# Four-layer decoder on one core: 128-column and 96-column TensorE products cut into column tiles of 64

## The reference

```python
# layer 0 attention: gates of 8 heads, from one small product
log_g = logsigmoid(x @ Wg + 6.906768)            # Wg: 256 x 8

# cross-attention of layers 0, 2 and 3: 16 heads, K=128, D_C=64, D_CQ=192, R=64
q_big  = einsum('bshk,hkq->bshq', hidden_q @ Wq.T, w_kc_q)   # rope on q_big in layers 0 and 2, not in 3
scores = einsum(q_big @ W_qr, kv_r @ W_kr)       # so W_qr . W_kr (192 x 64 per head) can be made first
attn   = softmax(scores); ctx_c = attn @ kv_r; out = (ctx_c @ w_kc_kv) @ Wo.T

# feed-forward of layers 1, 2, 3: the router
logits = x @ router                              # 256 x 16, 256 x 9, 256 x 8
```

## Time and profile before

| | |
|---|---|
| median of 3 runs | 1659.71 us |
| the profiled execution's own time | 1663.67 us |
| its span, first to last instruction | 1661.9 us |
| PE busy | 1621.5 us, 98% of the span |
| PE weight loads busy | 1098.9 us, 66% |
| DVE / ACT / POOL busy | 1114.3 / 750.1 / 239.8 us |
| mean granted TensorE clock | 0.994 |

### The profile page before, as it was taken

The page is one execution under the profiler, slowest core; times in us unless marked ns, Lnnn a source line. Parts: engine busy times, 40 slices in busy tenths (PEclk is TensorE's granted clock), DMA queues, the critical chain, the costliest instruction groups (busy, mean ns, idle before and its releaser), DMA issues.

```text
span 1661.9 us, 35781 instructions
## 1 busy us (share of the span) xinstructions
PE 1621.5 (98%) x15298; PEld 1098.9 (66%) x15298; DVE 1114.3 (67%) x1974; ACT 750.1 (45%) x1297; POOL 239.8 (14%) x429
## 2 busy tenths in 40 slices
PE   9999999999998899999999999999999999999998
PEld 5574377777755666654377777764566767777765
DVE  3726889999566753266889999535445289999633
ACT  2223466666313541143366666312444366666411
POOL 0011200000010312011200000010455000000030
PEclk9999999999999999999999999999999999999999
DMA  9302020000040011050020000060300220000010
GB/s 281 85 15 82 1 78 2 2 2 2 15 175 1 2 61 38 1 146 36 1 97 2 2 2 2 2 242 0 64 2 1 115 90 2 2 2 2 2 45 11
DMA packets 35522, 71.10 MB, mean 43 GB/s; under 512 B 25359, under 2 KB 29775, under 8 KB 31433
## 3 DMA queue, kind: packets, MB, share of 16 engines
q1 hardware_dynamic: 35240, 68.71, 12.6%
q10 hardware_dynamic: 126, 0.11, 0.0%
HBM read 68.36 MB, written 0.46 MB: 41 GB/s over the span
## 4 chain that ended last, share of the span: by engine, by line
PE 89%; DVE 6%; ACT 2%; POOL 1%; issue 1%; DMA 0%; DVEq 0%; POOLq 0%; ACTq 0%
PE ps L1124 14%; PE ps L1137 14%; PE ps L1037 13%; PE ps L361 9%; PE ps L1503 9%; PE ps L948 3%; PE ps L2601 3%; PE ps L1152 3%; PE ps L529 2%; PE ps L1963 2%; PE ps L958 1%; POOL arena L1797 1%; PE ps L2628 1%; PE ps L984 1%; PE ps L969 1%
## 5 line engine op out<-in xcount | busy, mean ns | idle before, releaser
L1238 ACT ACTIVATE arena<-ps,softmax_stats 128x1500 f32<-128x1500 f32 x168 | 254.0, 1512 | 195.4 <-DVE softmax_stats L1319 193.4
L1137 PEld LDWEIGHTS ps<-arena,ctx_pos 125*64 125x64 f32 x4608 | 222.3, 137 | 58.4 <-issue 56.8
L1124 PE MATMUL ps<-ident,arena 64*125 64x64 f32 x4032 | 239.6, 271 | 1.9 <-ACT arena L1238 1.6
L1137 PE MATMUL ps<-arena,ctx_pos 125*64 125x128 f32 (+1 forms) x4608 | 240.5, 262 | 0.0
L1124 PEld LDWEIGHTS ps<-ident,arena 64*125 64x125 f32 x4032 | 227.2, 186 | 17.0 <-issue 13.5
L1037 PE MATMUL ps<-ctx_feat,arena 64*128 64x500 f32 x1008 | 233.2, 596 | 0.0
L1245 ACT COPY arena<-ps 125x512 f32<-125x512 f32 x336 | 172.5, 599 | 78.3 <-PE ps L1124 78.3
L1317 DVE TENSOR_REDUCE softmax_stats<-ps 128x1 f32<-128x500 f32 x252 | 170.7, 678 | 51.8 <-PE ps L1037 51.7
L361 PE MATMUL ps<-arena 128*128 128x256 f32 x736 | 175.1, 384 | 5.6 <-DVE arena L726 1.7
L1330 DVE TENSOR_SCALAR arena<-arena,softmax_stats 128x1500 f32<-128x1500 f32 x168 | 168.3, 1002 | 5.9
L1503 PE MATMUL ps<-x_feat,arena 128*128 128x448 f32 (+1 forms) x416 | 166.2, 544 | 1.2 <-DVE arena L1615 1.2
(11 more groups left out here) (324 smaller groups left out, 1920.1 us busy)
## 6 DMA issues: line engine op xcount, KB each, us to landing
ctx_pos<-in_ctx SPq DMA_DIRECT2D x1, 2688.0 KB
arena<-in_L1f_gate SPq DMA_DIRECT2D x1, 2304.0 KB, 13.2
arena<-in_L1f_up SPq DMA_DIRECT2D x1, 2304.0 KB, 17.5
arena<-in_L1f_down SPq DMA_DIRECT2D x1, 2304.0 KB, 7.8
arena<-in_L0a_Wq SPq DMA_DIRECT2D x1, 2048.0 KB, 10.8
arena<-in_L0a_Wc SPq DMA_DIRECT2D x1, 2048.0 KB, 18.8
arena<-in_L0x_Wq SPq DMA_DIRECT2D x1, 2048.0 KB, 10.3
arena<-in_L0x_Wo SPq DMA_DIRECT2D x1, 2048.0 KB, 8.4
```

The source lines that it names most:

```text
L1124: m = nc.tensor.transpose(c.ps[0:LP, turn_bank(i, k, r), n * 64:(n + 1) * 64], probs[i % 2][e][rows, l * LP:(l + 1) * LP], c.ident[rows, r ...
L1137: m = nc.tensor.matmul(y[r * 64:(r + 1) * 64, lo:hi], c.ctx_pos[:, j, l, e, :], pT[i % 2][:, lo // 64:hi // 64, LT * e + l, :], start=(l = ...
L1238: nc.scalar.activation(probs[i % 2][e].rearrange("p (k l) -> p k l", k=3), sc[e], ACT.Exp, bias=low[:, i % 4, e:e + 1], accum_out=total[:, ...
```

## The change

Four edits. (1) The gates and the routers of layers 1 to 3: each product of 128 weight columns becomes two of 64 columns, one per sequence, into PSUM partitions 0 to 63 and 64 to 127. (2) `fold_kz` and `fold_wq`: the same. (3) `wide`: each product of 96 columns becomes one of 64 and one of 32 columns, in the order 64 (r = 0), 64 (r = 1), 32 (r = 0), 32 (r = 1); the semaphores count twice per g. (4) At g = 8 of layer 0's attention `weigh(7)` goes ahead of `out(6)`.

```diff
 # gates (and, with f.cols and bank 7, the routers where not mixing)
-                m = nc.tensor.matmul(c.ps[:, 0, j * GH:(j + 1) * GH], c.x_feat[:, k, 2 * j:2 * j + 2, :],
-                                     wg[:, k, :], start=(k == 0), stop=(k == KT - 1))
+                for e in range(2):
+                    m = nc.tensor.matmul(c.ps[e * TP:(e + 1) * TP, 0, j * GH:(j + 1) * GH], c.x_feat[:, k, 2 * j + e, :],
+                                         wg[:, k, :], start=(k == 0), stop=(k == KT - 1))
...
+            if g == GH:
+                weigh(g - 1)
             if g >= 2:
                 out(g - 2)
-            if 1 <= g <= GH:
+            if 1 <= g < GH:
                 weigh(g - 1)
...
 # wide(g)
-                    for r in range(2):
-                        rows = slice(r * 64, (r + 1) * 64)
-                        m = nc.tensor.matmul(c.ps[0:DH, wide_bank(g, r), (2 * i + e) * 64:(2 * i + e + 1) * 64],
-                                             wqr[rows, 4 * g + i, e * DH:(e + 1) * DH], wkr[rows, 4 * g + i, :],
-                                             start=True, stop=True)
-                        if i == 3 and e == 1:
-                            m.then_inc(*wide_mm[r].next())
+                    for lo, hi in ((0, 64), (64, DH)):
+                        for r in range(2):
+                            rows = slice(r * 64, (r + 1) * 64)
+                            m = nc.tensor.matmul(c.ps[lo:hi, wide_bank(g, r), (2 * i + e) * 64:(2 * i + e + 1) * 64],
+                                                 wqr[rows, 4 * g + i, e * DH + lo:e * DH + hi], wkr[rows, 4 * g + i, :],
+                                                 start=True, stop=True, tile_position=(r * 64, lo))
+                            if i == 3 and e == 1:
+                                m.then_inc(*wide_mm[r].next())
...
 # fold_kz; fold_wq in the same way
-                    m = nc.tensor.matmul(c.ps[:, 2 + g % 2, (h % 4) * 64:(h % 4 + 1) * 64], kcqT[:, e, h, :],
-                                         z[:, h, e, :], start=(e == 0), stop=(e == 1))
+                    for r in range(2):
+                        m = nc.tensor.matmul(c.ps[r * 64:(r + 1) * 64, 2 + g % 2, (h % 4) * 64:(h % 4 + 1) * 64],
+                                             kcqT[:, e, h, r * 64:(r + 1) * 64], z[:, h, e, :], start=(e == 0), stop=(e == 1))
...
-                    act.wait_ge(wide_mm[1].handle, wide_mm[1].at(h + 1))
+                    act.wait_ge(wide_mm[1].handle, wide_mm[1].at(2 * h + 2))
```

More of the change, by code:

```diff
@@ L1006, in fold_wq @@
                     at = k * 256 + (h % 4) * 64
-                    m = nc.tensor.matmul(c.ps[:, 4 + g % 2, at:at + 64], wqT[:, h, k * 128:(k + 1) * 128],
-                                         kz[g % 2][:, h % 4, :], start=True, stop=True)
+                    for r in range(2):
+                        m = nc.tensor.matmul(c.ps[r * 64:(r + 1) * 64, 4 + g % 2, at:at + 64],
+                                             wqT[:, h, k * 128 + r * 64:k * 128 + (r + 1) * 64],
+                                             kz[g % 2][:, h % 4, :], start=True, stop=True)
             m.then_inc(*fold_mm.next())
@@ L1266, in wide_out @@
             for r in range(2):
-                dve.wait_ge(wide_mm[r].handle, wide_mm[r].at(g + 1))
+                dve.wait_ge(wide_mm[r].handle, wide_mm[r].at(2 * g + 2))
                 nc.vector.tensor_copy(zr[:, g, r], c.ps[0:DH, wide_bank(g, r), :].rearrange("p (i n) -> p i n", i=4)).then_inc(*wide_in.next())
@@ L1276, in _ @@
             for g in range(2):
-                dve.wait_ge(wide_mm[0].handle, wide_mm[0].at(g + 1))
+                dve.wait_ge(wide_mm[0].handle, wide_mm[0].at(2 * g + 2))
                 dve.wait_ge(padded.handle, padded.at(1))
@@ L1484, in _ @@
             for k in range(KT):
-                m = nc.tensor.matmul(c.ps[:, 7, j * f.cols:(j + 1) * f.cols], c.x_feat[:, k, 2 * j:2 * j + 2, :],
-                                     wr[:, k, :], start=(k == 0), stop=(k == KT - 1))
+                if mixing:
+                    m = nc.tensor.matmul(c.ps[:, 7, j * f.cols:(j + 1) * f.cols], c.x_feat[:, k, 2 * j:2 * j + 2, :],
+                                         wr[:, k, :], start=(k == 0), stop=(k == KT - 1))
+                    continue
+                for e in range(2):
+                    m = nc.tensor.matmul(c.ps[e * TP:(e + 1) * TP, 7, j * f.cols:(j + 1) * f.cols], c.x_feat[:, k, 2 * j + e, :],
+                                         wr[:, k, :], start=(k == 0), stop=(k == KT - 1))
         m.then_inc(*logits.next())
```

## The result

The changed kernel took 1666.41 us (median of 5, 1663.95 to 1669.25), the kernel before in the same comparison 1661.06 us. The ratio is 1.0036, with a 95% interval of 1.0020 to 1.0053: slower by 6 us (3.3 to 8.8), where 8.8 were forecast. All ratios here leave out single executions far above the rest of their kernel, of which there are three: 1761.63 and 9272.55 us of wide_thirds and one of 1717.76 us of the kernel before; why they were so long, I do not know. The profiled execution took 1663.95 us, its span is 1662.2 us, at a mean granted clock of 0.998. The one of before had 0.994; the two spans differ by only 0.3 us, because the one of before spent more of its time at the lower clock. That is also why the span "near 1671" of the prediction was not seen. The stages are therefore compared where both have the full clock.

A forecast was written before the change was run, and what follows sets the result against it. The PE was taken as the bound, with 89% of the span on its chain. Terms -1.4 - 1.9 + 10.4 + 0.2 = +7.3 us, plus 1.7 for the clock, made +9.0 on 1659.71: 1668.5 us, range 1660.5 to 1682.

The forecast's parts named there:

- near 1671: Forecast span in us of the changed kernel's profiled execution: +9.0 on the span of 1661.9 before.
- The path: Whole kernel: the PE's list sets the time; in layers 0 and 2 a change of `wide`'s length goes through in full.
- The price of a run: Passes of one tile size followed by another size: 0.14 us per run, at least 0.1 of it for the size change.
- Rival 1: `wide`: the step between 64 and 32 columns is free, 1.1 us per g, sum -8.8, 1651 us; chance 0.15.
- 2: Rival on `wide`: twice as many size changes, 32 per g, 6.4 us per g, 1681 us in all; chance 0.13.
- Rival 3: `wide`: short runs cost 0.08 to 0.10 us, no further clock fall, 1661 to 1663 us; chance 0.12.
- Gates: Kernel start: 1.82 us becomes about 1.1, but the PE then idles 0.7 us for `tri`; gain 0, at most 0.1.
- weigh(7) ahead of out(6): Layer 0's attention: divide(7) is hidden under out(6), so the PE's 1.26 us idle ahead of out(7) goes; gain 1.4 us.
- Routers: Three routers: 1.80 us becomes 1.13 each, gain 0.6 to 0.7 each, 1.9 us in all.
- so that the wait behind `gate_up` does not take it back: Routers: the logits come as much earlier for DVE's top-k, so the 0.6 to 0.7 us gained each is kept.
- Folds and layer 3: Layer 3: `wide` loses 5.4 us, wq0 starts 4.1 later, the folds behind the Wq load give back 3.9; net +0.2.
- The clock: Layer 3's new `wide`, 8 us of short passes: one more fall to the lower clock, 1.7 us; up to three more in range.

The follow-up runs named there:

- wide_thirds: The changed kernel with the 96 columns of `wide` as three products of 32; ratio 1.0003 to the kernel before.
- wide_alone: The kernel before with only the new `wide` and its semaphore counts; ratio 1.0085.
- wide_whole: The changed kernel with `wide` as before, in 96-column products; 1654.19 us, ratio 0.9963 to the kernel before.
- wide_grouped: The changed kernel with all 64-column products of a g in `wide` first, then all 32-column ones, 2 runs per g; ratio 0.9974 to the kernel before.
- wide_by_head: The changed kernel with `wide` ordered by pair of heads, four 64-column products then four 32-column ones, 8 runs per g; ratio 1.0001 to the kernel before.
- order_alone: The kernel before with only weigh(7) ahead of out(6); ratio 0.9994.
- folds_alone: The kernel before with only the folds split; ratio 0.9982.
- thirds_02: The changed kernel with `wide` in three 32-column products in layers 0 and 2, uncut 96 columns in layer 3; ratio 0.9957 to the kernel before.
- thirds_3_late: The changed kernel with `wide` in three 32-column products in layer 3 only, and that layer's loads issued later; ratio 0.9987 to the kernel before.
- routers_alone: The kernel before with only the gates and the three routers split; ratio 0.9994.

## Why the prediction was right

- **The path.** That PE's list is what counts, and that nothing hides a longer `wide` in layers 0 and 2, held: 11.93 - 7.02 = 4.91 us per stage, twice 2.46. The total of wide_alone agrees.
- **The price of a run** was forecast as 0.14 us from runs in the trace of before, and measured 0.133 to 0.134 over three orders. `wide` came to 3.96 us per g instead of 4.1. wide_whole, wide_grouped and wide_by_head leave no other cause for the loss. The Trainium skill's rule that a change of tiling mode drains the TensorE (TensorEngine Tiling (Array Packing), Key Properties) holds for the step between 64 and 32 columns too; its price here is in these lines.
- **Rivals.** 1 and 2 fall: a free step would have given 1.1 us per g, twice the changes over 6. The gap stands behind every four passes. Rival 1's time for four tiles at once is real, though, for tiles of one size: 1.12 us in wide_thirds. Rival 3 was wrong in its price, 0.08 to 0.10 us per run, and right in its other half, that no fall of the clock is added.
- **Gates.** Gain none; the idle ahead of L530 is 0.47 us, not 0.7.
- **weigh(7) ahead of out(6).** weigh(7) to the end of out(7) is 128.37 - 120.28 = 8.09 us; before, out(6) began at 120.31 and 129.93 - 120.31 = 9.6 us later the next line ran. Gain 1.5, forecast 1.4. That is a reading of the timeline; order_alone's ratio does not settle it (for its time at the same clock see the last section).
- **Routers.** The lines themselves gained 0.66, 0.77 and 0.77 us, 2.2 in all, forecast 1.9. The step "so that the wait behind `gate_up` does not take it back" failed in layer 2: a wait of 1.92 us for DVE and POOL took back most of the 0.77 and of the 1.67 that the missing fall of the clock gave. The net gain there is 0.4 us, and in all 0.66 + 0.4 + 0.77 = 1.8. That this is near 1.9 is luck.
- **Folds and layer 3.** Net 0.0, forecast +0.2. The 3.9 us behind the load are seen alone in folds_alone, and the wait that swallows what is won ahead of it in folds_alone and wide_whole.
- **The clock** was the other wrong step: "I add one such fall, 1.7 us". In the 8 us of `wide` in layer 3 it stayed up:

```profile
1300.90:1308.80 7.90, 7.86 (x128) 5.37 (x128) 1.28 (x2) 1.28 (x2) 0.15 (x1) 1.00 0.88 325
```

Nor did the other executions have more falls: the mean granted clock of the five of the changed kernel is 0.9970, that of 96 of the kernel before 0.9954; for wide_alone it is 0.9955 over six, where its kernel before had 0.9949. One fall of 3.4 us to half the clock would be 0.001 less.

The measured terms, 4 x 2.46 + 0.0 - 1.5 - 1.8 = +6.5 us, agree with the +6.0 of the ratio within its interval. The forecast sum of +9.0 was too high by the 1.7 of the clock, by 4 x 0.14 for the size of `wide`, and by smaller parts. The forecast time of 1668.5 us looks closer to 1666.41 than it is, since the kernel before also took 1.35 us more in this comparison than in the one that the forecast started from.

## What to carry to other kernels

Count the changes of tile size before you cut a product into tiles: here each cost 0.13 us, as much as four or five passes of 64 columns, and the prediction's sum breaks even at 0.065. Do not alternate the pieces of a width with a rest, as 96 = 64 + 32. Grouping them by size helped (2.09 us instead of 3.96) but lost against no cut at all (1.50); only equal tiles beat that (1.12 and 1.28), and in the long `wide` of layer 3 they ended in a stop that cost more than they had won. And ask on which side of a load a gain lies: ahead of it, it turns into a wait, which may take the clock down as well; filled with products that nothing reads, the wait no longer cost the clock. The same question holds for other engines: behind layer 2's router POOL set the pace, and what the PE had won ahead of it was lost again.

## What the runs showed of the hardware that was not expected

- Six tiles of 64 rows and 32 columns run at once: the first six passes start within 33 ns, and 96 passes of 64 moving columns take 1.12 us, 11.7 ns per pass (1.28 us in `wide(1)`).
- The PE can stop with no semaphore awaited, it seems because it outruns its instructions. 187 pairs of weight load and matmul in 2.1 us were followed by a stop of 4.98 and 5.38 us while a 2 MB load ran, and of 1.79 us when that load was held back. The page shows it as idle by "issue".
- Waits of 1.95, 2.20 and 3.59 us of the PE (thirds_02, wide_whole, thirds_3_late) were followed by 3.4 us at 1.2 GHz, waits of 0.20 to 0.90 us for the same load in four other kernels were not. In the stop of 5.38 us the clock fell for 13.6 us:

```profile
1301.00:1314.60 13.60, 11.47 (x115) 7.40 (x116) 1.39 (x3) 0.75 (x2) 0.00 (x0) 0.50 0.55 231
```

- A long stretch of short passes with gaps between them did not bring the clock down, in two kernels. Not every fall has a wait ahead of it: right before the one behind layer 2's old router the PE was busy 3.07 of 3.40 us. In the four kernels with the old router that fall stands in the profile, in the ten with the split one it does not, one profile each.
- The times of one kernel spread over 3 to 12 us, and the falls make most of it. Over 96 executions of the kernel before, a straight line of time against mean granted clock falls 1.1 us per 0.001 and leaves a scatter (standard deviation) of 0.9 us, where the times have 2.4. At the same clock by that line, an estimate, order_alone is 1.8 us faster than the kernel before, folds_alone 3.6 faster, wide_alone 14.4 slower; routers_alone comes out level, since the line counts the fall that the split router takes away as clock and leaves the wait behind it. The changed kernel is 7.6 us slower at the same clock: the 6 us of the ratio hold some gain from its fewer falls.
